# Clearing on ScalarE inside the first scan steps, and separate load semaphores, in the prelude of a recurrent block kernel

## What is computed

```
def step(h, xt):                       # scan over 256 steps
    m = concat([xt, h]) @ weight + bias          # weight: 256 x 256
    c = tanh(m[:, 128:])
    g = sigmoid(m[:, :128] + 1.0)
    return g * h + (1 - g) * c
x = x + scan(step, cond, x)
x = x + block(x, cond, w_q, ..., w_ada, b_ada)
```

## Time and profile before

| what | us |
|---|---|
| median of three runs | 463.85 (463.63 to 463.85) |
| span of the profiled execution, first to last instruction | 461.8 |
| median less that span | 2.05 |
| start of the first matmul of step 0 (L804) in the span | 13.20 |
| clear of `V` on GpSimd (L608) | 4.16 to 8.10 |

### The profile page before, as it was taken

How to read it: one execution, slowest core, us unless ns; L and a number is a source line. 1 busy time by engine, 2 the same in 40 slices (tenths; PEclk the granted TensorE clock), 3 DMA queues, 4 the chain that set the end, 5 groups by cost and what they waited for, 6 DMA issues and landing times.

```text
span 461.8 us, 14117 instructions
## 1 busy us (share of the span) xinstructions
PE 375.0 (81%) x5296; PEld 253.9 (55%) x5296; DVE 304.8 (66%) x1938; ACT 231.7 (50%) x1025; POOL 78.5 (17%) x151
## 2 busy tenths in 40 slices
PE   1999899898857896857898999979599899778832
PEld 1755676566746675746666766636344446446510
DVE  5454444576777776777776676653842378699883
ACT  2123422325335425335446455645688878953952
POOL 7000000012000012000012000032210124266580
PEclk9999999999999999999999999985759989995966
DMA  7200840002000000000000000000000000000102
GB/s 179 62 1 4 181 95 3 2 3 48 1 1 3 1 4 1 2 2 1 2 3 3 1 4 1 2 2 2 3 2 3 1 2 4 1 2 1 23 1 68
DMA packets 9114, 8.42 MB, mean 18 GB/s; under 512 B 1276, under 2 KB 7694, under 8 KB 9047
## 3 DMA queue, kind: packets, MB, share of 16 engines
q1 hardware_dynamic: 8950, 7.26, 7.0%
q0 software_dynamic: 96, 0.26, 0.2%
HBM read 6.45 MB, written 1.08 MB: 16 GB/s over the span
## 4 chain that ended last, share of the span: by engine, by line
PE 56%; DVE 22%; ACT 12%; issue 5%; POOL 2%; DMA 1%; SPq 0%; DVEq 0%; ACTq 0%; POOLq 0%
PE zb L804 21%; PE tb L927 6%; PE zb L782 4%; DVE prod_hi L1569 4%; PE tb L751 4%; ACT state L1265 3%; PE firsts L1098 3%; PE firsts L983 2%; ACT prd L1421 2%; PE tb L898 2%; PE zb L1078 2%; PE firsts L967 2%; ACT state L1268 2%; PE zb L788 2%; PE firsts L804 2%
## 5 line engine op out<-in xcount | busy, mean ns | idle before, releaser
L804 PEld LDWEIGHTS zb<-prod_hi,whh 128*128 128x128 f16 x1920 | 73.7, 106 | 89.9 <-DVE prod_hi L1569 85.8
L1265 ACT ACTIVATE state<-zb 128x8 f32<-128x8 f32 x240 | 42.7, 178 | 152.9 <-PE zb L804 152.4
L804 PE MATMUL zb<-prod_hi,whh 128*128 128x8 f16 x1920 | 91.0, 171 | 34.7 <-DVE prod_hi L1569 34.0
L1569 DVE SCALAR_TENSOR_TENSOR prod_hi<-state 128x16 f16<-128x16 f32 x255 | 44.7, 175 | 83.0 <-ACT state L1268 80.1
L804 PE MATMUL zb<-prod_lo,whh 128*128 128x8 f16 x960 | 63.7, 172 | 0.0
L1575 DVE TENSOR_TENSOR prod_lo<-prod,prod_hi 128x16 f16<-128x16 f32 x255 | 44.7, 175 | 8.7
L1421 ACT ACTIVATE prd<-zb 128x640 f32<-128x640 f32 x64 | 42.2, 712 | 7.8 <-PE zb L1078 7.2
L804 PEld LDWEIGHTS zb<-prod_lo,whh 128*128 128x128 f16 x960 | 44.5, 107 | 0.8
L1571 DVE SCALAR_TENSOR_TENSOR prod<-state 128x16 f32<-128x16 f32 x256 | 43.3, 169 | 0.3 <-ACT state L1268 0.3
L1268 ACT ACTIVATE state<-zb 128x16 f32<-128x16 f32 x240 | 42.8, 178 | 0.0
L1577 DVE SCALAR_TENSOR_TENSOR state<-prod 128x8 f32<-128x8 f32 x256 | 40.8, 159 | 0.0
(11 more groups left out here) (378 smaller groups left out, 708.6 us busy)
## 6 DMA issues: line engine op xcount, KB each, us to landing
mod<-ada_rows SPq DMA_DIRECT2D x4, 768.0 KB, 11.8
resid<-in_x_dram SPq DMA_DIRECT2D x6, 128.0 KB, 3.7
ffz<-shift_rows SPq DMA_DIRECT2D x4, 131.0 KB, 3.3
out_dram<-state SPq DMA_DIRECT2D x8, 64.0 KB, 2.1
out_dram<-early SPq DMA_DIRECT2D x8, 64.0 KB, 2.1
yy<-in_L_cond_w_ada_dram SPq DMA_DIRECT2D x1, 384.0 KB
early<-in_L_cond_weight_dram SPq DMA_DIRECT2D x2, 128.0 KB
resid<-in_x_dram POOLq DMA_DIRECT2D x2, 128.0 KB, 3.5
```

The lines of the kernel that those rows point to most:

```text
L804: i = pe.matmul(z_bank(t, k)[:, NB * (t % CH):NB * (t % CH) + NB], whh[:, half, p, k, :], src[:, NB * p:NB * p + NB], start=False, stop=Fa ...
L1265: act.activation(r[:, 24:32], z_bank(t, 1)[:, k:k + NB], ACT.Tanh, scale=-1.0 / ZS)
L1569: dve.scalar_tensor_tensor(prod_hi[:, :], r[:, 16:32], 1.0, r[:, 0:16], ALU.add, ALU.mult).then_inc(hi_ready, 1)
```

## The change

GpSimd no longer loads chunk 0 of `x`, and no longer clears `V` and `O`. The two loads are now issued by ScalarE, ahead of everything else it does. The clearing is done by a new ScalarE worker, `zeros`: nine copies of 128x512 from one zero column into `V`, two copies of 128x512 into `O`, one of 128x256 for the constant column, one per tick from tick 2 on. VectorE waits for the last of them before the first values are written (tick 126).

The weight comes in one load instead of two, and `load_scan` is split into `load_w0`, `load_cond` and `load_b0`, each waited for by those that need it. ScalarE makes the four high parts of `whh` straight from the loaded weight; VectorE makes the four low parts with one fused instruction each; the scaled intermediate `whs` is gone. ScalarE copies the transposed chunk 0 in two pieces: the first 16 steps (`xT_first`, which TensorE waits for before L770) and the other 48 (`xT_sb`, waited for in tick 1).

```diff
@@ sync @@
-            sp.dma_start(w0h[:, :], w0[D:2 * D, :]).then_inc(load_scan, 16)
-            sp.dma_start(condr[:, :], cond).then_inc(load_scan, 16)
-            sp.dma_start(b0row[:, :], row(b0)).then_inc(load_scan, 16)
-            sp.dma_start(w0x[:, :], w0[0:D, :]).then_inc(load_scan, 16)
+            sp.dma_start(early[:, 0, :, :].rearrange("p (a b) d -> p a (b d)", a=2),
+                         w0.rearrange("(a p) n -> p a n", p=D)).then_inc(load_w0, 16)
+            sp.dma_start(condr[:, :], cond).then_inc(load_cond, 16)
+            sp.dma_start(b0row[:, :], row(b0)).then_inc(load_b0, 16)
@@ gpsimd @@
-            for slot in range(2):
-                tile_dma(pool, x, resid, 0, slot, False).then_inc(load_x0, 16)
...
-            settled(pool.memset(V[:, :, :, :, :], 0.0))
-            pool.memset(V[:, :, :, :, HD:HD + 1], C_HEAD)
-            pool.memset(O[:, :, :, (NC - 1) * P:NC * P], 0.0).then_inc(pool_init, 1)
@@ tensor @@
-            pe.wait_ge(load_scan, 64)
+            pe.wait_ge(load_cond, 16)
...
             pe.wait_ge(x_split, 1)
-            pe.wait_ge(xT_sb, 1)
+            pe.wait_ge(xT_first, 1)
             first_x_part()
...
+                pe.wait_ge(xT_sb, 1)
                 yield from x_part(0)
...
-                pe.wait_ge(pool_init, 1)
@@ scalar @@
+            for slot in range(2):
+                tile_dma(act, x, resid, 0, slot, False).then_inc(load_x0, 16)
+
+            act.wait_ge(load_w0, 16)
+            for k, off in ((1, 0), (0, D)):
+                for p in range(2):
+                    s = ZS * (1.0, 0.5)[k] / (4, 2)[p]
+                    i = act.activation(whh[:, 0, p, k, :], w0h[:, off:off + D], ACT.Copy, scale=s)
+            i.then_inc(w_high, 1)
             act.wait_ge(condT_ps, 1)
...
-            copy_xT(0)
+            act.wait_ge(xT_ps, 1)
+            copy_xT(0, 0, FIRST).then_inc(xT_first, 1)
+            copy_xT(0, FIRST, CH).then_inc(xT_sb, 1)
...
+            def zeros(now):
+
+                yield from at_ticks(now, 2)
+                act.wait_ge(zero_set, 1)
+                flat = V.rearrange("p b k h d -> p (b k h d)")
+                for k in range(9):
+                    i = act.activation(flat[:, 512 * k:512 * k + 512], view(zero[:, 0:1], [0, 512]), ACT.Copy)
+                    yield
...
+                for k in range(2):
+                    act.activation(last[:, 4 * k:4 * k + 4, :], view(zero[:, 0:1], [0, 4], [0, P]), ACT.Copy)
+                    yield
+                act.wait_ge(act_done, mark)
+                act.activation(V[:, :, :, :, HD:HD + 1].rearrange("p b k h d -> p (b k h) d"),
+                               view(zero[:, 0:1], [0, NB * 2 * NH], [1, 1]), ACT.Copy, bias=C_HEAD)\
+                    .then_inc(v_zeros, 1)
@@ vector @@
+            dve.wait_ge(load_w0, 16)
+            for k, off in ((0, D), (1, 0)):
+                dve.tensor_scalar(w0s[:, k, :], w0x[:, off:off + D], ZS * (1.0, 0.5)[k], None, ALU.mult)
+            dve.wait_ge(load_b0, 16)
...
-                dve.tensor_scalar(whs[:, 0, k, :], w0h[:, off:off + D], s / 4, None, ALU.mult)
-                dve.tensor_scalar(whs[:, 1, k, :], w0h[:, off:off + D], s / 2, None, ALU.mult)
...
-            settled(dve.tensor_copy(whh[:, 0], whs[:, :, :, :]))
-            dve.tensor_tensor(whh[:, 1], whs[:, :, :, :], whh[:, 0], ALU.subtract).then_inc(w_split, 1)
...
+            dve.wait_ge(w_high, 1)
+            for k, off in ((1, 0), (0, D)):
+                for p in range(2):
+                    s = ZS * (1.0, 0.5)[k] / (4, 2)[p]
+                    i = dve.scalar_tensor_tensor(whh[:, 1, p, k, :], w0h[:, off:off + D], s,
+                                                 whh[:, 0, p, k, :], ALU.mult, ALU.subtract)
+            i.then_inc(hi_ready, 1)
```

More of the change, by code:

```diff
@@ L230, in ugrnn_block_kernel @@
         w0s = sb("w0s", [P, 2, D])
-        whs = early[:, 1, :, :].rearrange("p (a b) d -> p a b d", a=2)
+        zero = sb("zero", [P, 1])
         whh = sb("whh", [P, 2, 2, 2, D], F16)
@@ L364, in ugrnn_block_kernel @@
         NSCAN = sum(1 for g in GROUPS if g[2] < 256)
-        load_scan, load_x0 = sem("load_scan"), sem("load_x0")
+        load_w0, load_cond, load_b0, load_x0 = sem("load_w0"), sem("load_cond"), sem("load_b0"), sem("load_x0")
         load_x, load_rest = sem("load_x"), sem("load_rest")
@@ L370, in ugrnn_block_kernel @@
         consts16 = sem("consts16")
-        pool_init = sem("pool_init")
-        x_split, w_split = sem("x_split"), sem("w_split")
+        zero_set, halves, v_zeros = sem("zero_set"), sem("halves"), sem("v_zeros")
+        x_split, w_high = sem("x_split"), sem("w_high")
+        xT_first = sem("xT_first")
         condT_ps, condT_sb = sem("condT_ps"), sem("condT_sb")
@@ L606, in _ @@
             pool.memset(neg_half[:, :], -0.5)
-            pool.memset(half_[:, :], 0.5)
-            settled(pool.memset(V[:, :, :, :, :], 0.0))
-            pool.memset(V[:, :, :, :, HD:HD + 1], C_HEAD)
-            pool.memset(O[:, :, :, (NC - 1) * P:NC * P], 0.0).then_inc(pool_init, 1)
+            pool.memset(half_[:, :], 0.5).then_inc(halves, 1)
             def times(dst, a, b):
@@ L1249, in _, with copy_xT @@
             act.activation(condT[:, :], tb[:, 0, 0:NB], ACT.Copy).then_inc(condT_sb, 1)
-            def copy_xT(c):
-                act.wait_ge(xT_ps, c + 1)
-                first = xT[:, STEPS // NC * NB * c + batch_of(c, 0, 0):][:, 0:1]
+            def copy_xT(c, lo=0, hi=CH):
+                first = xT[:, STEPS // NC * NB * c + NB * lo + batch_of(c, 0, 0):][:, 0:1]
                 s = batch_of(c, 0, 1) - batch_of(c, 0, 0)
-                act.activation(view(first, [2, NJ], [s, 2], [NB, CH]),
-                               xT_bank(c).rearrange("p (j s t) -> p j s t", j=NJ, s=2),
-                               ACT.Copy).then_inc(xT_sb, 1)
-            copy_xT(0)
+                return act.activation(view(first, [2, NJ], [s, 2], [NB, hi - lo]),
+                                      xT_bank(c).rearrange("p (j s t) -> p j s t", j=NJ, s=2)[:, :, :, lo:hi],
+                                      ACT.Copy)
+            act.wait_ge(xT_ps, 1)
+            copy_xT(0, 0, FIRST).then_inc(xT_first, 1)
+            copy_xT(0, FIRST, CH).then_inc(xT_sb, 1)
             def step(t):
@@ L1269, in step @@
                                scale=1.0 / ZS).then_inc(step_in, 1)
+            def zeros(now):
[5 more added lines that the diff above has]
+                    yield
+                done[0] += 1
+                i.then_inc(act_done, 1)
+                mark = done[0]
+                last = O[:, :, :, (NC - 1) * P:NC * P].rearrange("p j i q -> p (j i) q")
+                for k in range(2):
[5 more added lines that the diff above has]
+                    .then_inc(v_zeros, 1)
             def prepare(now):
@@ L1284, in prepare @@
                     yield from at_ticks(now, 26 + 4 * c)
-                    copy_xT(c)
+                    act.wait_ge(xT_ps, c + 1)
+                    copy_xT(c).then_inc(xT_sb, 1)
                 yield from at_ticks(now, 37)
@@ L1516, in _ @@
             tails = [tail(n) for n in range(len(PAIRS))]
-            run(step, [prepare, tokens, attention, *tails])
+            run(step, [zeros, prepare, tokens, attention, *tails])
         @block.vector
@@ L1539, in _ @@
             dve.memset(onesh[:, :], 1.0)
-            dve.wait_ge(load_scan, 64)
+            dve.memset(zero[:, :], 0.0).then_inc(zero_set, 1)
+            done_(dve.memset(prod[:, NB:2 * NB], 0.0))
+            dve.wait_ge(load_w0, 16)
+            for k, off in ((0, D), (1, 0)):
+                dve.tensor_scalar(w0s[:, k, :], w0x[:, off:off + D], ZS * (1.0, 0.5)[k], None, ALU.mult)
+            dve.wait_ge(load_b0, 16)
             for k, off in ((0, D), (1, 0)):
                 s = ZS * (1.0, 0.5)[k]
-                dve.tensor_scalar(w0s[:, k, :], w0x[:, off:off + D], s, None, ALU.mult)
-                dve.tensor_scalar(whs[:, 0, k, :], w0h[:, off:off + D], s / 4, None, ALU.mult)
-                dve.tensor_scalar(whs[:, 1, k, :], w0h[:, off:off + D], s / 2, None, ALU.mult)
                 done_(dve.tensor_scalar(b0s[:, k, :], b0row[:, off:off + D], s, (0.0, s)[k],
@@ L1550, in _ @@
             dve.tensor_tensor(b0h[:, 1], b0s[:, :, :], b0h[:, 0], ALU.subtract).then_inc(x_split, 1)
-            settled(dve.tensor_copy(whh[:, 0], whs[:, :, :, :]))
-            dve.tensor_tensor(whh[:, 1], whs[:, :, :, :], whh[:, 0], ALU.subtract).then_inc(w_split, 1)
-            done_(dve.memset(prod[:, NB:2 * NB], 0.0))
             dve.wait_ge(condT_sb, 2)
             settled(dve.tensor_scalar(prod[:, 0:NB], state[:, 0:NB], 2.0, None, ALU.mult))
-            done_(dve.tensor_copy(prod_hi[:, :], prod[:, :]))
-            settle()
+            settled(dve.tensor_copy(prod_hi[:, :], prod[:, :]))
             dve.tensor_tensor(prod_lo[:, :], prod[:, :], prod_hi[:, :], ALU.subtract)\
                 .then_inc(lo_ready, 1)
```

(6 more changed lines are left out.)

## The result

Nine runs of the changed kernel have a median of 458.78 us (456.94 to 462.50), nine of the kernel before beside them 463.30 (461.89 to 463.85); the ratio is 0.9904 (95%: 0.9886 to 0.9923), a gain of 4.4 us (3.6 to 5.3). A second set gave 457.34 against 462.84, ratio 0.9893 (0.9873 to 0.9913), a gain of 5.0 us (4.0 to 5.9). The forecast was 458.9, between 457.4 and 460.8.

A forecast was written before the change was run, and what follows sets the result against it. The start was taken as bound by VectorE, stalled by GpSimd's clears; with chunk 0's landing last, step 0 moves from 13.20 to 8.19, so 461.8 - 5.0 + 2.05 gives 458.9 us, range 457.4 to 460.8.

The forecast's parts named there:

- The stall of VectorE: VectorE's scalings before step 0: GpSimd's clears stall them, 3.9 us of the chain, and the stall goes entirely.
- L: Landing time of chunk 0 of `x` at the start: taken as 4.5 us, between 3.4 and 5.7.
- the sum by bytes: Chunk 0's landing from bytes: 0.52 MB at 215 GB/s, 2.4 us after first bytes near 1.8, so about 4.2.
- Rival B: Start: loads become the bound by sharing the DMA engines; chunk 0 at 6.5, step 0 at 10.2, 460.9 us; chance 0.08.
- the lower bound: Earliest landing of chunk 0: second issue at 1.34 plus 2.1 of a lone 64 KB store, 3.4 us.
- The line behind L: TensorE from chunk 0's landing to step 0: transposes 1.12, short copy 0.40, input part 2.10, 3.69 us in sum.
- The lines from W: From the weight's landing (W, 3.9 us) through VectorE and ScalarE: bias split at 5.3, `hi_ready` at 7.2, not last.
- The clears in the gaps: ScalarE, ticks 2 to 13: twelve clearing copies fit gaps of some 1.06 us and cost nothing.
- The sum: Whole kernel: span 461.8 - 5.0 = 456.8, plus 2.05 between span and median, 458.9 us.
- Rival E: Tail: TensorE's granted clock varies, one stretch at the lower level worth up to 3.3 us; chance 0.05.
- C: Start: GpSimd is not what stalls VectorE; scalings stay long, step 0 at 11.3, 462.0 us; chance 0.04.
- D: Ticks 2 to 13: long clearing copies push each next `tanh`; at 1.6 us each, 465.3 us; chance 0.03.

The follow-up runs named there:

- the one with both edits: Changed kernel with the bias matmuls put ahead of the input matmuls and chunks 1 to 3 of `x` issued only when chunk 0 has landed: 456.35 us, ratio 0.9871.

## Why the prediction was right, and where it was not

**The stall of VectorE** was read rightly: the scalings are short, and putting the clears back lengthens them again. The forecast of what the clears alone were worth rests on the same steps and came out (10.15).

**The landing of chunk 0, L, is the term that was mis-sized.** "I take 4.5"; it was 5.5. With all loads under way the rate was not under the 215 that was taken: the stretches after show 241 and 225 GB/s:

```profile
2.00:4.00 2.00, 0.00 (x0) 0.00 (x0) 0.09 (x1) 1.38 (x2) 0.14 (x3) 1.00 0.84 241
4.00:6.00 2.00, 0.73 (x3) 0.64 (x4) 1.72 (x10) 0.94 (x6) 0.00 (x0) 1.00 0.78 225
```

The bytes were a part of it. From 1.8 to 5.5 us some 0.86 MB moved, and the sum had 0.52, with "more if chunk 1 gets in between"; chunks 1 to 3 took their share from the start. But with chunks 1 to 3 late the engines had only the bytes of the sum, and chunk 0 still came at 4.99, not at the 4.2 that the sum gave: those bytes moved at a mean of 189 GB/s, where 215 was taken, and were there at 4.55 (0.35 us), and the transposes started 0.44 behind the last of them, a step that the sum by bytes put at nothing. The other 0.55 are chunks 1 to 3. So three terms of L were too small. Rival B had the crowd as its mechanism, at a harder size (6.5). The 4.35 of chunk 0 by itself is near the 4.5 by chance: that 4.5 was meant for chunk 0 beside the weight. The other bound, 5.3 from issue and landing rows, and 5.7 from TensorE's old wait, were the better ones. The 2.1 of the lower bound was not of a store "alone": the row is a median of eight, and the last four of them go out within 2.5 us.

**The line behind L** was right: 3.69 forecast, 3.76 measured, with 0.40 for the short copy. Step 0 was forecast at 8.19 and came at 9.30; of the miss of 1.11, 1.04 are L.

**The lines from W** were right: W 3.9 forecast and 3.9 measured, VectorE's fused lows 0.89 for 1.1, `hi_ready` at 6.83 for 7.2. `hi_ready` stays off the line in every variant. The bias split, the other end of these lines, was last in two: with the clears back on GpSimd, and with the weight held back for chunk 0.

**The clears in the gaps** cost nothing, as forecast: a copy of 128x512 took 0.63 for 0.60. The one-column copy took 0.68, where "less" than 0.60 was said; it is still inside the gap of 1.06.

**The sum** therefore came nearer than its parts by luck, through two effects that it did not have. Forecast 5.0; at step 0 there were 3.9; GpSimd's loads gone give 0.3 outside the span ("2.05 between span and median" was carried over unchanged); step 26 gives 0.3 more. That is 4.5, and 4.4 was measured in the first set, 5.0 in the second. That the time lies in the range is not luck: the range had L up to 5.7.

**Rival E** was dismissed on a wrong ground. "the three runs agree within 0.22 us" was true of those three; the spans of the 38 later runs of before that were made beside the experiments lie between 458.6 and 463.9, and the changed kernel's part behind the scan went from 165.5 to 170.4. Nothing here ties the long part to the change. Over all profiles it lies between 165.2 and 170.4; the upper end came in the changed kernel's first profile and in the one with both edits, which has the same stretch of 17 us at the lower level, and not in the changed kernel's second. The three lowest mean clocks on record belong to three kernels, and each is the longest execution of its kernel in its set: 460.7 at 0.926 for the changed kernel (the next is 457.6), 458.4 at 0.926 for the one with both edits (455.7), 463.9 at 0.927 for the kernel before (460.6). So such an execution costs some 3 us more than the next longest, near the 3.3 at which the rival priced one stretch; why one comes is open.

**C and D** did not happen: each of the first two scalings takes 0.22, and of the steps with a clear none differs from its twin in the kernel before by more than 0.02 us.

## What to carry to other kernels

Read a late engine's timeline beside GpSimd's: if a VectorE instruction takes ten times its twin and ends with a GpSimd instruction, suspect that it waits for it, and test it by moving the GpSimd work; here moving the clears to idle gaps of a third engine removed the wait. When a load becomes the last thing, count all bytes that share the time up to its landing, not only those issued ahead of it, add the time from the last byte to the start of whoever waits (some 0.4 us here), and let later loads wait for it. Judge a change of the start at the first step that it releases, in the profile, before trusting a total that varies by more than the effect.

## What the runs showed of the hardware that was not expected

- Loads issued by GpSimd lengthen the time outside the span: 2.08 to 2.23 us in the 58 runs of the experiments with them (before, and two variants), 1.76 to 1.93 in 44 of 45 runs without, and 2.06 in one.
- From the end of chunk 0's last packet to the start of the transposes it takes 0.35 to 0.55 us in the nine profiles in which ScalarE issued it, and 0.78 to 0.98 in the four in which GpSimd did.
- Four small 16-bit matmuls mixed in pairs with f32 ones add 1.05 us, and 0.56 in a block of their own.
- ScalarE's copy into single elements 72 bytes apart (the constant column of `V`, one in 18 elements of 4 bytes) takes 0.68 us for 256 elements, and a contiguous one 0.63 for 512; both read one zero column:

```profile
L1283 ACT ACTIVATE V<-zero 128x512 f32<-128x512 f32 x9 | 5.7, 630 | 0.0
...
L1293 ACT ACTIVATE V<-zero 128x256 f32<-128x256 f32 x1 | 0.7, 682 | 0.0
```

- Step 26 is 0.31 us shorter in every variant, and ScalarE's program differs from before's in all of them, also where the clears stayed on GpSimd. In the kernel before, ScalarE's first `tanh` of that step starts 0.36 us after TensorE is done. Why is open.
